# The third block of a causal convolution as four accumulating matrix products

## The chip, the cores and the metric

The kernel runs on one core of one Trainium2 chip. The metric is the device time in microseconds of one execution; the time of a kernel is the median of its runs. TensorE, VectorE, ScalarE and GpSimd work side by side, each through its own queue in order, and wait for one another by semaphores; SyncE issues the transfers.

## The reference

16 sequences of 64 tokens with 128 channels attend to 1601 context tokens each, go through a state-space layer and an MLP, and then through a mixture of eight experts. The change lies in the state-space layer, of which this matters:

```
v = layernorm(x, ln1_w, ln1_b)
zxbcdt = v @ in_proj_w.T                    # 128 -> z 256 | xBC 384 | dt 4
dt  = softplus(dt_raw + dt_bias)
xBC = sum(conv_w[:, k] * pad(xBC)[:, k:k+L] for k in range(4)) + conv_b   # causal, per channel
xBC = silu(xBC)                             # xs 256 | B 64 | C 64
h_t = exp(dt * A) h_{t-1} + dt * xs_t B_t ;  y_t = h_t C_t + D * xs_t
out = rmsnorm(y * silu(z)) @ out_proj_w.T
```

All arithmetic of this layer is in 32-bit floats. The channels of xBC come in three blocks of 128: two of xs, and a third with B in its first 64 rows and C in its last 64.

## The kernel before

The program has three blocks, one after the other: the attention (to about 400 us), the state-space layer with its MLP (function `mamba_mlp`, 400 to 475 us) and the experts. Each block writes out by hand, engine by engine, what the engine does in which order. `win` holds the input projection transposed (columns 0 to 255 z, 256 to 639 xBC, 640 to 643 dt), `vecs` per-channel columns (taps at `V_CW`, bias at `V_CB`), and `rows` a few vectors laid out over all 128 partitions.

In the second block the 1024 tokens are handled as two halves `h` of 512, each eight sequences of 64. Channels lie on the partitions. For each half, TensorE turns v (`turn_v`, L1159), ScalarE copies it to `vT` with scale and bias (L1354), and TensorE makes three products of 512 columns, one for each block of channels (`project_x`, L1164), each into one bank of the accumulator memory, named by `MM_BANK[h][c]`. ScalarE reads the bank, multiplies by the last tap, adds the bias and writes `conv` (`last_tap`, L1360); VectorE adds the three earlier taps, each shifted by one more token within its sequence, reading the bank again (`convolve`, L1541); ScalarE takes the silu into `xbc` (`conv_silu`, L1378), for the third block in two parts of 64 rows. TensorE's products for z (L1199, banks `Z_BANK`) feed `gate_silu` (L1383).

VectorE's order is: convolve (0,0) and (0,1), four small steps for dt, convolve (0,2), six steps, convolve (1,0), four steps, convolve (1,1), the decay split into three bf16 parts (L1590 to L1596), convolve (1,2), and then the train of `scan` (L1602), `mixed` (L1614, L1619) and `gated` (L1632). TensorE turns the decay parts (L1228) into banks 2 and 3, ScalarE copies them to `decayT` (L1400), TensorE spreads them over the partitions (`spread`, L1212), ScalarE copies the spread (`decay_all`, L1409) and VectorE scans it. `overlap` (L1240) multiplies B by C, `turn_x` (L1221) turns xs, `skipped` (L1254) starts the sums of y in banks 0 and 1 (first half) or 2 and 3 (second half) of the slots `YA_SLOT`, `state` (L1265) adds to them, and `project_out` (L1276, L1281) makes the output and the sums of squares.

Products called `idle` (L139) compute something that nobody reads; they only keep TensorE at work at chosen places. All their records have the line L139. `s["mm"]` counts finished projections, `s["tap"]` last taps, `s["conv"]` convolutions, `s["silu"]` silus, `s["zin"]` and `s["zsil"]` the gate's products and silus, `s["dp"]` parts of the decay, `s["dpt"]` their turning, `s["dpc"]` the copies to `decayT`, `s["bc"]` and `s["bcc"]` spreads and their copies, `s["ya"]` finished halves of y.

Of the kernel before, what the change touches and what calls it, by code (L numbers as in the profile page):

```python
# [5 lines left out]
ALU = mybir.AluOpType  # L6
ACT = mybir.ActivationFunctionType
# [4 lines left out]
P = 128  # L12
B, LQ, LK = 16, 64, 1601
# [27 lines left out]
V_CW, V_CB, V_D, V_NW, V_FCB = 9, 21, 24, 26, 28  # L41
# [1 line left out]
NV = 36  # L43

R_BV, R_BO, R_PB, R_ALOG, R_DTB = 0, 128, 256, 384, 388
NR = 392

MH = 4
E, NH, HT = 8, 3, 114
# [92 lines left out]
def attention(nc, A, keep):  # L142


    with ExitStack() as ctx:
# [97 lines left out]
        s_laid = sem("s_laid")  # L243
# [147 lines left out]
        def _(pool):  # L391
# [94 lines left out]
            for c in range(2):  # L486
                pool.tensor_scalar(keep.skip[:, c, :], keep.ident[:], keep.vecs[:, V_D + c:V_D + c + 1], None,
                                   ALU.mult).then_inc(s_laid, 1)
            for c in range(2):
                pool.tensor_scalar(keep.wout[:, c, :], keep.wout[:, c, :], keep.vecs[:, V_NW + c:V_NW + c + 1], None,  # L490
                                   ALU.mult).then_inc(s_laid, 1)
# [534 lines left out]
def mamba_mlp(nc, A, keep):  # L1026

    with ExitStack() as ctx:
# [9 lines left out]
        rows, vecs, ident = keep.rows, keep.vecs, keep.ident  # L1038
# [6 lines left out]
        vT = sb("vT", [P, T])  # L1045
        stats, mean_var, rstd12, var12 = keep.stats, keep.mean_var, keep.rstd12, keep.var12
        rstd = sb("rstd2", [P, NT])
        conv = sb("conv", [P, 4, T])
# [37 lines left out]
        def tok(t):  # L1086
            return slice(t * P, t * P + P)

        def half(h):
            return slice(512 * h, 512 * h + 512)  # L1090
# [5 lines left out]


        MM_BANK = ((2, 3, 4), (5, 0, 1))
        Z_BANK = ((4, 7), (6, 5))
        FC_BANK = ((2, 3, 4, 6), (7, 0, 1, 5))  # L1100
        TURN_BANK = (4, 6)

# [32 lines left out]
        def _(pe):  # L1135
# [27 lines left out]
            def project_x(h, c):  # L1163
                pe.matmul(bank(MM_BANK[h][c]), keep.win[:, 256 + P * c:256 + P * c + P], vT[:, half(h)],  # L1164
                          start=True, stop=True).then_inc(s["mm"], 1)

            def idle(b, times):
                spend(pe, bank(b), keep.w_hi[:, 0, 0, 0:P],
                      keep.w_hi[:, 1].rearrange("p g c -> p (g c)")[:, 0:512], times)
# [7 lines left out]
            project_x(0, 0)  # L1177
            project_tokens()
            project_x(0, 1)
            project_x(0, 2)  # L1180
            idle(1, 3)
            turn_v(0, 1, 1)
            idle(6, 4)
# [2 lines left out]
                last = pe.matmul(bank(6)[:, MH * t:MH * t + MH], vT[:, tok(t)], keep.win[:, 640:644],  # L1186
                                 start=True, stop=True)
            last.then_inc(s["dtp"], 1)
            for c in range(3):
                project_x(1, c)  # L1190
            for h in range(2):
                for c in range(2):

                    if c == 0:
                        pe.wait_ge(*((s["conv"], 3), (s["dts"], 2))[h])
                    elif h:
                        idle(3, 3)
                        pe.wait_ge(s["conv"], 4)
                    pe.matmul(bank(Z_BANK[h][c]), keep.win[:, P * c:P * c + P], vT[:, half(h)],  # L1199
                              start=True, stop=True).then_inc(s["zin"], 1)  # L1200

# [20 lines left out]
                last.then_inc(s["xt"], 1)  # L1222


            idle(3, 12)
            pe.wait_ge(s["dp"], 3)
            for t in range(NT):
                last = pe.matmul(ps[0:3 * MH, 1, tok(t)], decay_parts[:, t, :], ident_bf[:], start=True, stop=True)  # L1228
            last.then_inc(s["dpt"], 1)
            idle(0, 4)  # L1230
            pe.wait_ge(s["dpc"], 1)
            spread(0)

            def overlap(h):
# [10 lines left out]
            def skipped(h2):  # L1245

                if h2:
                    pe.wait_ge(s["bcc"], 4)
                else:
                    pe.wait_ge(s["conv"], 6)  # L1250
                pe.wait_ge(s["silu"], 4 * h2 + 2)
                for b in range(2):
                    for c in range(2):
                        pe.matmul(y_out(h2, b, c), keep.skip[:, c, :],  # L1254
                                  xbc[:, c, half(h2)].rearrange("p (t b q) -> p t b q", b=2, q=LQ)[:, :, b, :],
                                  start=(c == 0), stop=False, skip_group_check=True)
# [89 lines left out]
        def _(act):  # L1346
# [10 lines left out]
            def last_tap(h, c):  # L1357

                act.wait_ge(s["mm"], 3 * h + c + 1)
                nc.scalar.activation(conv[:, c, half(h)], bank(MM_BANK[h][c]), ACT.Identity,  # L1360
                                     bias=vecs[:, V_CB + c:V_CB + c + 1],
                                     scale=vecs[:, V_CW + 4 * c + 3:V_CW + 4 * c + 4]).then_inc(s["tap"], 1)
# [10 lines left out]
            def conv_silu(h):  # L1373

                for c in range(4):
                    act.wait_ge(s["conv"], 3 * h + min(c, 2) + 1)
                    m, src = (P, conv[:, c, half(h)]) if c < 2 else (64, conv[64 * (c - 2):64 * (c - 1), 2, half(h)])
                    nc.scalar.activation(xbc[0:m, c, half(h)], src, ACT.Silu).then_inc(s["silu"], 1)  # L1378

            def gate_silu(h):  # L1380
                for c in range(2):
# [4 lines left out]
            act.wait_ge(s["dts"], 4)  # L1386
            nc.scalar.activation(dt_e[:], dt_a[:], ACT.Exp).then_inc(s["dte"], 1)
            nc.scalar.activation(a_exp[:], rows[:, R_ALOG:R_ALOG + MH], ACT.Exp).then_inc(s["dte"], 1)
            last_tap(0, 2)
            last_tap(1, 0)  # L1390
            act.wait_ge(s["dts"], 5)
            nc.scalar.activation(dt_l[:], dt_u[:], ACT.Ln).then_inc(s["dte"], 1)
            last_tap(1, 1)
            last_tap(1, 2)
            act.wait_ge(s["dts"], DT_LAST - 1)
            nc.scalar.activation(decay[:], decay[:], ACT.Exp, bias=keep.marks[:, M_FIRST:M_FIRST + 1],
                                 scale=-1.0).then_inc(s["dts"], 1)
            conv_silu(0)
            act.wait_ge(s["dpt"], 1)
            nc.scalar.copy(decayT[:], ps[0:3 * MH, 1, :]).then_inc(s["dpc"], 1)  # L1400
            gate_silu(0)
            act.wait_ge(s["ones"], 1)
            for c in range(4):
# [42 lines left out]
        def _(dve):  # L1446
# [85 lines left out]

            def convolve(h, c):

                dve.wait_ge(s["tap"], 3 * h + c + 1)
                src = bank(MM_BANK[h][c]).rearrange("p (b q) -> p b q", q=LQ)
                dst = conv[:, c, half(h)].rearrange("p (b q) -> p b q", q=LQ)
                cw = vecs[:, V_CW + 4 * c:V_CW + 4 * c + 4]
                for k in range(1, 4):
                    settle()  # L1540
                    ins = dve.scalar_tensor_tensor(out=dst[:, :, k:], in0=src[:, :, 0:LQ - k],  # L1541
                                                   scalar=cw[:, 3 - k:4 - k], in1=dst[:, :, k:],
                                                   op0=ALU.mult, op1=ALU.add)
                    if k < 3:
                        count(ins)
                    else:
                        ins.then_inc(s["conv"], 1)
# [17 lines left out]
            step(dve.tensor_scalar(dt_a[:], dt_x[:], -1.0, None, ALU.mult))  # L1565
            step(dve.tensor_tensor(dt_a[:], dt_a[:], dt_x[:], ALU.min))
            step(dve.tensor_scalar(dt[:], dt_x[:], 0.0, None, ALU.max))
            convolve(0, 2)
            dve.wait_ge(s["dte"], 2)
            step(dve.tensor_scalar(dt_u[:], dt_e[:], 1.0, None, ALU.add))  # L1570
            step(dve.tensor_scalar(dt_a[:], dt_u[:], -1.0, None, ALU.add))
# [15 lines left out]
            for part in range(3):  # L1587
# [6 lines left out]
                    rest = decay_rest  # L1594
                else:
                    dve.tensor_copy(to, rest[:]).then_inc(s["dp"], 1)  # L1596
            convolve(1, 2)


            def scan(c):  # L1600
# [412 lines left out]
def program(nc, A, out):  # L2013
    with ExitStack() as ctx:
        def sb(name, shape, dt=F32):
            return ctx.enter_context(nc.sbuf_tensor("keep_" + name, shape, dt))

        keep = Keep()
        keep.x = sb("x", [P, NT, P])
        keep.ident = sb("ident", [P, P])  # L2020
        keep.marks = sb("marks", [P, 5])
        keep.vecs = sb("vecs", [P, NV])
        keep.rows = sb("rows", [P, NR])
        keep.iota = sb("iota", [P, E])
        keep.sums = sb("sums", [P, GH, T])
        keep.wo = sb("wo", [P, P])
        keep.win = sb("win", [P, 644])
        keep.wout = sb("wout", [P, 2, P])
        keep.wfc = sb("wfc", [P, 4 * P])
        keep.wproj = sb("wproj", [P, 4, P])  # L2030
        keep.w_hi = sb("w_hi", [P, E, 2, NH * HT], BF16)
        keep.w_lo = sb("w_lo", [P, E, 2, NH * HT], BF16)
        keep.delta = sb("delta", [P, 8, LQ])
        keep.skip = sb("skip", [P, 2, P])
        keep.sel = sb("sel", [3 * MH, MH, P], BF16)
        keep.ident_bf = sb("ident_bf", [P, P], BF16)
        keep.stats = sb("stats", [P, NT, 6])
        keep.mean_var = sb("mean_var", [P, NT, 2])
        keep.rstd12 = sb("rstd12", [P, 2, NT])
        keep.var12 = sb("var12", [P, NT])  # L2040
        attention(nc, A, keep)
        keep.tT = sb("tT", [P, T])
        keep.bgu = sb("bgu", [HT, E, 2, NH])
        keep.b2 = sb("b2", [E, P])
        keep.cent = sb("cent", [P, E])
        keep.cent_sq = sb("cent_sq", [P, E])
        keep.ones = sb("ones", [P, P])
        keep.norms = sb("norms", [P, NT])
        keep.dots = sb("dots", [P, 5 * E])
        keep.t_hi = sb("t_hi", [P, T], BF16)  # L2050
        keep.t_lo = sb("t_lo", [P, T], BF16)
        keep.w2 = sb("w2", [HT, E, NH, P])
        mamba_mlp(nc, A, keep)
        experts(nc, A, keep, out)

def lay_out(a):
# [20 lines left out]
    def cols(v):  # L2079
# [6 lines left out]
        cols(np.repeat(g["attn_D_param"], 64)), cols(g["attn_norm_w"]), cols(g["attn_fc_b"]),  # L2086
        np.where(marks[:, M_LOW:M_LOW + 1] > 0, bq.reshape(P, G), 0).astype(f)], 1)
    rows = np.concatenate([g["xattn_bv"], g["xattn_bo"], g["attn_proj_b"], g["attn_A_log"],
                           g["attn_dt_bias"]])[None]
    c = np.ascontiguousarray  # L2090
    return {
        "x": c(g["x"].reshape(T, P)),
# [36 lines left out]
```

## Time and profile before

| what | value |
|---|---|
| median of 3 runs | 590.32 us (589.23, 590.91, 590.32) |
| the profiled execution's own time | 589.35 us |
| its span, first to last instruction | 587.5 us |
| mean granted TensorE clock | 0.976 of full |
| busy: TensorE, VectorE, ScalarE, GpSimd | 89%, 71%, 65%, 55% |

The span is what the trace covers; 1.85 us of the execution's time lie around it. The trace shows for each engine when each instruction started and how long it took, and, where an engine stood idle, whose semaphore ended the wait. The granted clock is given as a share of TensorE's full 2.4 GHz; 0.50 is its lower level, 1.2 GHz.

### The profile page before, as it was taken

The page shows a single profiled execution, that of the slowest core. Times are in us where ns is not written, and L with a number is a line of the kernel's source. Part 1 is how long each engine was busy: PE and PEld are TensorE (multiplying, and loading weights), DVE is VectorE, ACT ScalarE, POOL GpSimd, SP SyncE. Part 2 cuts the span into 40 slices and gives each one's busy share as a digit, 9 for nine tenths or more (in the row PEclk, how much of TensorE's full clock was granted, in tenths as well). Part 3 has the DMA queues.
Part 4 walks back from the last instruction along what each step waited for, and adds up shares of the span by engine and source line. Part 5 has one row for each costly group of instructions (what it writes and reads, how often), then busy time and mean ns, then how long its engine had stood idle before and what let it go on. Part 6 is the DMA issues. An engine that isn't in the chain of part 4 may idle for free. (4 is left out here: it accounts for less than half of the span.)

```text
span 587.5 us, 18795 instructions
## 1 busy us (share of the span) xinstructions
PE 523.7 (89%) x7876; PEld 338.8 (58%) x7876; DVE 419.7 (71%) x751; ACT 381.1 (65%) x704; POOL 323.8 (55%) x197
## 2 busy tenths in 40 slices
PE   3988999999999889999999897998899868999996
PEld 1634555565565555665665564664367635777775
DVE  6277887788788786798798698536887576455555
ACT  4873667678677667677777677873672525666662
POOL 2697967558657556559558099303000035667772
PEclk9987999999999998999999999999899989999999
DMA  6897766684694682864762775002000000000001
GB/s 210 128 137 127 163 83 103 105 113 82 96 125 69 96 107 56 127 85 90 116 88 39 112 113 109 5 2 99 1 2 1 1 1 1 2 2 0 0 0 37
DMA packets 16409, 41.62 MB, mean 71 GB/s; under 512 B 3990, under 2 KB 6814, under 8 KB 16218
## 3 DMA queue, kind: packets, MB, share of 16 engines
q1 hardware_dynamic: 15592, 40.09, 41.9%
q8 instruction: 59, 0.97, 0.8%
q10 hardware_dynamic: 740, 0.42, 0.2%
q14 instruction: 18, 0.15, 0.1%
HBM read 19.70 MB, written 0.52 MB: 34 GB/s over the span
## 5 line engine op out<-in xcount | busy, mean ns | idle before, releaser
L896 DVE TENSOR_REDUCE half_max<-wide 128x2 f32<-128x802 f32 x256 | 241.8, 989 | 55.7 <-PE wide L582 51.9
L822 ACT ACTIVATE probs<-score 128x512 f32<-128x512 f32 (+1 forms) x416 | 225.8, 596 | 74.0 <-PE score L633 73.6
L653 PE MATMUL sums<-probs,values 128*32 128x192 f32 (+3 forms) x3328 | 133.6, 280 | 5.4 <-issue 5.3
L653 PEld LDWEIGHTS sums<-probs,values 128*32 128x32 f32 (+1 forms) x3328 | 87.5, 110 | 58.2 <-issue 30.4
L582 PE MATMUL wide<-k_stack,q_cur 48*128 48x401 bf16 x512 | 88.1, 340 | 12.6 <-ACT k_full L804 6.1
L633 PE MATMUL score<-q_cur,k_stack 50*128 50x128 bf16 (+1 forms) x1664 | 83.3, 219 | 9.5 <-ACT probs L822 4.7
L413 POOL TENSOR_TENSOR ctx_hi<-ctx_in,one 128x1601 bf16<-128x1601 f32 x15 | 42.9, 2859 | 76.5 <-PE wide L504 67.7
L1864 POOL TENSOR_TENSOR hid_lo<-hid_e,hid_hi 114x512 bf16<-114x512 f32 x47 | 54.2, 1158 | 36.6 <-ACT hid_hi L1892 35.5
L633 PEld LDWEIGHTS score<-q_cur,k_stack 50*128 50x128 bf16 (+1 forms) x1664 | 52.1, 95 | 35.4 <-issue 11.7
L1992 DVE SCALAR_TENSOR_TENSOR hid_e<-gu,keep_bgu,gate 114x512 f32<-114x512 f32 x48 | 35.9, 751 | 42.1 <-ACT gate L1905 40.7
L425 POOL TENSOR_TENSOR k_hi<-k_full,one 128x1601 bf16<-128x1601 f32 x15 | 42.9, 2857 | 41.9 <-ACT k_full L804 33.6
L1905 ACT ACTIVATE gate<-gu,gate_bias 114x512 f32<-114x512 f32 x48 | 32.9, 688 | 37.5 <-PE gu L1833 35.0
L416 POOL TENSOR_TENSOR ctx_lo<-ctx_in,ctx_hi 128x1601 bf16<-128x1601 f32 x15 | 48.6, 3242 | 1.2
L428 POOL TENSOR_TENSOR k_lo<-k_full,k_hi 128x1601 bf16<-128x1601 f32 x15 | 48.6, 3238 | 1.2
L582 PEld LDWEIGHTS wide<-k_stack,q_cur 48*128 48x128 bf16 x512 | 25.0, 94 | 39.1 <-DVE half_max L896 16.3
L1831 PE MATMUL gu<-keep_t_hi,keep_w_hi 128*114 128x512 bf16 x96 | 37.5, 390 | 6.6 <-DVE hid_e L1992 6.6
L804 ACT ACTIVATE k_full<-wide,keep_vecs 128x802 f32<-128x802 f32 x26 | 24.2, 930 | 25.6 <-PE wide L504 25.6
L892 DVE COPY values<-wide 128x896 f32<-128x896 f32 (+1 forms) x28 | 28.7, 1025 | 15.4 <-PE wide L504 15.4
L1833 PE MATMUL gu<-keep_t_hi,keep_w_lo 128*114 128x512 bf16 x96 | 37.1, 387 | 0.0
L1832 PE MATMUL gu<-keep_t_lo,keep_w_hi 128*114 128x512 bf16 x96 | 37.1, 386 | 0.0
L502 PE MATMUL wide<-wkv_hi,ctx_hi 128*128 128x128 bf16 x182 | 33.4, 225 | 2.9 <-DVE half_max L896 2.9
L1812 PE MATMUL down<-w_hi,hid_hi 114*128 (+1 forms) x192 | 33.8, 219 | 1.1 <-DVE hid_lo L2001 1.1
(310 smaller groups left out, 889.1 us busy)
## 6 DMA issues: line engine op xcount, KB each, us to landing
k_stack<-k_hi SPq DMA_DIRECT2D x64, 204.0 KB, 6.4
ctx_in<-in_ctx SPq DMA_DIRECT2D x56, 200.1 KB, 6.3
k_stack<-k_lo SPq DMA_DIRECT2D x32, 204.0 KB, 8.6
ctx_in<-in_wgu SPq DMA_DIRECT2D x16, 171.0 KB, 4.8
keep_w<-in_w SPq DMA_DIRECT2D x1, 1368.0 KB
ctx_in<-in_ctx SPq DMA_DIRECT2D x1, 800.5 KB, 8.2
keep_x<-in_x SPq DMA_DIRECT2D x1, 512.0 KB, 6.8
out<-keep_x SPq DMA_DIRECT2D x2, 256.0 KB, 2.4
```

The costliest lines, as they stand in the source:

```text
L413: pool.tensor_tensor(ctx_hi[:, n, 0:LK], ctx_in[:, n, :], one[:].to_broadcast([P, LK]), ALU.mult).then_inc(s_splithi, 1)
L416: pool.tensor_tensor(ctx_lo[:, n, 0:LK], ctx_in[:, n, :], ctx_hi[:, n, 0:LK], ALU.subtract).then_inc(s_split, 1)
L425: pool.tensor_tensor(k_hi[:, 0:LK], k_full[:, 0:LK], one[:].to_broadcast([P, LK]), ALU.mult).then_inc(s_khi, 1)
L428: pool.tensor_tensor(k_lo[:, 0:LK], k_full[:, 0:LK], k_hi[:, 0:LK], ALU.subtract).then_inc(s_klo, 1)
L582: last = pe.matmul(wide[:, w, 512 * p:512 * p + CH], q_cur[half:half + TERM, b % NQ, g].rearrange("p h q -> p (h q)"), k_stack[half:half + ...
L633: last = pe.matmul(score[0:m, (2 * step + p) % NSCORE, P * g:P * g + P], k_stack[half:half + TERM + 2, n, g, k * P:k * P + m], q_cur[half: ...
L653: last = pe.matmul(sums[32 * g:32 * g + 32, first * LQ:(first + heads) * LQ], values[0:m, n, k, VW * g + 2 * c:VW * g + 2 * c + 32], probs ...
L822: nc.scalar.activation(probs[0:m, step % NPROB, :].rearrange("r (g p c) -> r p g c", g=G, p=2)[:, p], score[0:m, (2 * step + p) % NSCORE, ...
L896: dve.tensor_reduce(half_max[:, b % 2, :, u // 4, u % 4], wide[:, w, :].rearrange("p (c k) -> p c k", c=2)[:, :, 0:CH], AX.X, ALU.max).the ...
L1831: pe.matmul(o, hi, t_hi[:, half], start=True, stop=False)
L1832: pe.matmul(o, hi, t_lo[:, half], start=False, stop=False)
L1864: pool.tensor_tensor(hid_lo[:, par, h, n, :], hid[:, n, :], hid_hi[:, par, h, n, :], ALU.subtract).then_inc(s["lo"], 1)
```

## The change

The third block of channels (B and C) is no longer convolved by ScalarE and VectorE. A new tensor `win_taps` holds four copies of its projection weights, each multiplied by one tap per output channel; GpSimd makes it in the attention block. TensorE then forms the convolved block itself: one product with the last tap over all 512 columns, and three that add the earlier taps, reading tokens shifted by one, two and three inside each sequence (504, 496, 488 columns). The silu reads that bank directly and adds the bias. The counts of `tap` and `conv` become two per half, and what waited for them is renumbered.

As bank 4 and bank 1 now hold the convolved blocks until the silus have read them, the first gate product moves from bank 4 to bank 3, the turned decay parts go to two groups of rows of bank 2 alone (and are copied in two instructions), the first skip products wait for the eighth silu instead of the sixth convolution, and the unread products go to bank 2 where they went to bank 3, ten of them instead of twelve ahead of the decay's turning. `rows` grows by 512 columns for the taps.

```diff
-NR = 392
+R_CW = 392
+NR = 904
...
+            pool.tensor_tensor(keep.win_taps[:], keep.win[:, 512:512 + P].unsqueeze(1).to_broadcast([P, 4, P]),
+                               keep.rows[:, R_CW:R_CW + 4 * P].rearrange("p (k c) -> p k c", k=4),
+                               ALU.mult).then_inc(s_laid, 1)
...
-        Z_BANK = ((4, 7), (6, 5))
+        Z_BANK = ((3, 7), (6, 5))
...
+            def convolve_states(h):
+
+                out = bank(MM_BANK[h][2])
+                by_batch = out.rearrange("p (b q) -> p b q", q=LQ)
+                tokens = vT[:, half(h)].rearrange("p (b q) -> p b q", q=LQ)
+                pe.matmul(out, keep.win_taps[:, 3, :], vT[:, half(h)], start=True, stop=False, skip_group_check=True)
+                for back in range(1, 4):
+                    last = pe.matmul(by_batch[:, :, back:], keep.win_taps[:, 3 - back, :], tokens[:, :, 0:LQ - back],
+                                     start=False, stop=(back == 3), skip_group_check=True)
+                last.then_inc(s["mm"], 1)
...
-            project_x(0, 2)
+            convolve_states(0)
...
-            for c in range(3):
+            for c in range(2):
                 project_x(1, c)
+            convolve_states(1)
             for h in range(2):
                 for c in range(2):
                     if c == 0:
-                        pe.wait_ge(*((s["conv"], 3), (s["dts"], 2))[h])
+                        pe.wait_ge(*((s["conv"], 2), (s["dts"], 2))[h])
                     elif h:
-                        idle(3, 3)
-                        pe.wait_ge(s["conv"], 4)
+                        idle(2, 3)
+                        pe.wait_ge(s["conv"], 3)
...
-            idle(3, 12)
+            idle(2, 10)
             pe.wait_ge(s["dp"], 3)
             for t in range(NT):
-                last = pe.matmul(ps[0:3 * MH, 1, tok(t)], decay_parts[:, t, :], ident_bf[:], start=True, stop=True)
+                at = 32 * (t // 4)
+                last = pe.matmul(ps[at:at + 3 * MH, 1, tok(t % 4)], decay_parts[:, t, :], ident_bf[:],
+                                 start=True, stop=True)
             last.then_inc(s["dpt"], 1)
             idle(0, 4)
-            pe.wait_ge(s["dpc"], 1)
+            pe.wait_ge(s["dpc"], 2)
...
-                    pe.wait_ge(s["conv"], 6)
+                    pe.wait_ge(s["silu"], 8)
...
             def conv_silu(h):
                 for c in range(4):
-                    act.wait_ge(s["conv"], 3 * h + min(c, 2) + 1)
-                    m, src = (P, conv[:, c, half(h)]) if c < 2 else (64, conv[64 * (c - 2):64 * (c - 1), 2, half(h)])
-                    nc.scalar.activation(xbc[0:m, c, half(h)], src, ACT.Silu).then_inc(s["silu"], 1)
+                    if c < 2:
+                        act.wait_ge(s["conv"], 2 * h + c + 1)
+                        nc.scalar.activation(xbc[:, c, half(h)], conv[:, c, half(h)], ACT.Silu).then_inc(s["silu"], 1)
+                        continue
+                    rows = slice(64 * (c - 2), 64 * (c - 1))
+                    act.wait_ge(s["mm"], 3 * h + 3)
+                    nc.scalar.activation(xbc[0:64, c, half(h)], bank(MM_BANK[h][2])[rows], ACT.Silu,
+                                         bias=vecs[rows, V_CB + 2:V_CB + 3]).then_inc(s["silu"], 1)
...
-            last_tap(0, 2)
             last_tap(1, 0)
...
-            last_tap(1, 2)
...
-            nc.scalar.copy(decayT[:], ps[0:3 * MH, 1, :]).then_inc(s["dpc"], 1)
+            for h in range(2):
+                nc.scalar.copy(decayT[:, half(h)], ps[32 * h:32 * h + 3 * MH, 1, 0:512]).then_inc(s["dpc"], 1)
...
-            convolve(0, 2)
...
-            convolve(1, 2)
```

## Rows read from the trace of the kernel before

**Rows 1.** The page: span and instructions.

```profile
span 587.5 us, 18795 instructions
```

**Rows 2.** Timeline of TensorE, head of the second block: start, duration, instruction, idle before.

```profile
407.39 0.81 PE L139 MATMUL ps<-keep_w_hi 128*128 128x512 bf16 x3
409.13 1.15 PE L1159 MATMUL ps<-keep_ident,v 128*128 128x128 f32 x4 [0.93 <-DVE v L1483]
412.95 2.82 PE L1164 MATMUL ps<-vT,keep_win 128*128 128x512 f32 x6
418.46 1.43 PE L1199 MATMUL ps<-vT,keep_win 128*128 128x512 f32 x2 [2.68 <-DVE conv L1541]
419.68 3.31 PE L1199 MATMUL pt<-vT,keep_win 128*128 128x512 f32 x4
427.02 0.61 PE L1228 MATMUL ps<-keep_ident_bf,decay_parts 128*12 128x128 bf16 x8
455.20 0.61 PE L1159 MATMUL ps<-keep_ident,v 128*128 128x128 f32 x4
```

**Rows 3.** Timeline of VectorE, the same stretch.

```profile
416.13 2.27 DVE L1541 SCALAR_TENSOR_TENSOR conv<-ps,keep_vecs,conv 128x504 f32<-128x504 f32 x3 [1.11 <-ACT conv L1360]
425.94 0.18 DVE L1596 CAST decay_parts<-decay_rest 128x32 bf16<-128x32 f32 x1
426.04 2.27 DVE L1541 SCALAR_TENSOR_TENSOR conv<-ps,keep_vecs,conv 128x504 f32<-128x504 f32 x3
430.14 1.23 DVE L1602 TENSOR_TENSOR_SCAN gain<-decay_all,keep_delta 128x512 f32<-128x512 f32 x1 [1.83 <-ACT decay_all L1409]
```

**Rows 4.** Windows of 1 us: busy time of the engines, then the granted clock.

```profile
420.00:421.00 1.00, 1.00 (x2) 0.35 (x2) 0.96 (x2) 0.98 (x2) 0.00 (x0) 0.50 0.00 0
...
422.00:423.00 1.00, 1.00 (x3) 0.24 (x2) 0.86 (x6) 0.12 (x1) 0.00 (x0) 0.72 0.00 0
```

**Rows 5.** Timeline of ScalarE.

```profile
427.67 1.00 ACT L1400 CAST decayT<-ps 12x1024 bf16<-12x1024 f32 x1 [0.83 <-PE ps L1228]
428.58 0.58 ACT L1383 ACTIVATE zg<-ps 128x512 f32<-128x512 f32 x1
429.07 0.57 ACT L1383 ACTIVATE zg<-pt 128x512 f32<-128x512 f32 x1
431.56 2.32 ACT L1378 ACTIVATE xbc<-conv 128x512 f32<-128x512 f32 x4
455.59 1.84 ACT L1434 ACTIVATE conv<-ps,keep_vecs 128x512 f32<-128x512 f32 x3
```

**Rows 6.** One line's records: duration least, median, most, in ns.

```profile
L1164 PE MATMUL ps<-vT,keep_win x12: 592/592/676, 404.4 to 415.2; 128*128 128x512 f32 x12
```

**Rows 7.** Timeline of TensorE, the train of scans and states, and one later row.

```profile
431.62 1.89 PE L1254 MATMUL ps<-xbc,keep_skip 128*128 128x256 f32 x8
433.44 0.44 PE L1212 MATMUL ps<-decayT,keep_sel 12*64 12x64 bf16 x16
435.84 0.69 PE L1265 MATMUL ps<-mix,keep_sums 64*64 64x64 f32 x32
458.16 1.13 PE L1323 MATMUL pt<-vT,keep_wfc 128*128 128x512 f32 x2 [1.49 <-ACT vT L1354]
```

**Rows 8.** Timeline of VectorE, the same stretch.

```profile
436.67 1.29 DVE L1632 TENSOR_TENSOR y<-ps,zg 128x512 f32<-128x512 f32 x2
443.99 0.16 DVE L1637 TENSOR_SCALAR rms<-ps 128x4 f32<-128x4 f32 x1 [2.11 <-PE ps L1281]
```

**Rows 9.** Timeline of GpSimd at the end of the attention block.

```profile
357.94 1.27 POOL L484 TENSOR_TENSOR keep_delta<-keep_ident 128x512 f32<-128x512 f32 x1
```

**Rows 10.** Load of the rows: issues, size, us from issue to landing.

```profile
keep_rows<-in_rows SPq DMA_DIRECT2D x1, 196.0 KB, 10.3
```

**Rows 11.** Windows of 2 us after that load: last the transfer share and GB/s.

```profile
68.00:70.00 2.00, 2.00 (x32) 1.03 (x28) 0.15 (x2) 1.38 (x3) 1.92 (x2) 1.00 0.58 120
70.00:72.00 2.00, 1.59 (x30) 0.79 (x22) 2.00 (x3) 1.59 (x4) 2.00 (x1) 1.00 0.01 3
```

More of the change, by code:

```diff
@@ L1533, in convolve @@
             def convolve(h, c):
-                dve.wait_ge(s["tap"], 3 * h + c + 1)
+                dve.wait_ge(s["tap"], 2 * h + c + 1)
                 src = bank(MM_BANK[h][c]).rearrange("p (b q) -> p b q", q=LQ)
@@ L2029, in program @@
         keep.wfc = sb("wfc", [P, 4 * P])
+        keep.win_taps = sb("win_taps", [P, 4, P])
         keep.wproj = sb("wproj", [P, 4, P])
@@ L2088, in lay_out @@
     rows = np.concatenate([g["xattn_bv"], g["xattn_bo"], g["attn_proj_b"], g["attn_A_log"],
-                           g["attn_dt_bias"]])[None]
+                           g["attn_dt_bias"], g["attn_conv_w"].reshape(3, P, 4)[2].T.reshape(-1)])[None]
     c = np.ascontiguousarray
```

## The prediction

> **What bounds the kernel now.** The page gives a span of 587.5 us [rows 1] and TensorE busy 89% of it, but such shares are means over three stages, and the change touches only the middle one, the state-space layer and its MLP (400 to 475 us). The chain of waits is no help here: it ends at the block boundary at 474.97 us, so I read the timelines of the engines one beside the other, looking for which wait ends last.
>
> TensorE's timeline of the head of the stage [rows 2]: it has issued the second half's products by 415.7, then idles 2.68 us for conv (VectorE's third convolution, which begins late, at 416.13, because ScalarE's last tap of that block stands behind the Exp [rows 3]). Just after it resumes at 418.46 the granted clock is half: 0.50 of full speed in the slice from 420, and 0.72 as a mean in that from 422, when it is back [rows 4]. That is the 1.2 GHz level. The records of the gate products show it: four take 3.31 us, where six of the same shape took 2.82 [rows 2]. The low stretch, some 3.4 us from about 419.1 to 422.6, costs 1.7 us of matmul work. Then come twelve spare products and only at 427.02 the transposes of the decay. VectorE had finished the three parts of the decay at 426.12 [rows 3] (the semaphore reads little later), so it did not set the start of these transposes; TensorE itself did. From them ScalarE copies decayT (427.67), makes the gate, copies the first spread (429.55 to 430.11), and the scan begins at 430.14 [rows 3, 5].
>
> From the scan on, VectorE has no gap until 441.87 and each of its steps stands on the last. The end of this stretch, the first request for the rms at 443.99, waits for TensorE's output products [rows 8]. So two things set the stage's end: when the transposes of decay start, and then the train of scans, mixes and states.
>
> **The head: what is removed, what is added.** Removed from VectorE are two convolutions of three steps, 2.27 us each (2.19 from start to the next start) [rows 3]; from ScalarE two last taps of about 0.7 us. The second of the two convolutions, 426.04 to 428.31, lay before VectorE's wait until 430.14, so it is worth nothing. The first stood in the decay's own path, and with its wait of 1.11 us held the next steps from 415.01 to 418.32 (416.13 + 2.19). They now begin when ScalarE's a_exp is done, 415.37 and a handover, say 415.42. That is 2.90 us earlier: convolution (1,0) ends near 419.1, the three parts of decay near 423.2. ScalarE follows: it has a table load, Ln, a table load and Exp in the same order; its silus end near 423.9.
>
> Added on TensorE: a half's third product was one float product of 512 columns (two records, 0.85 us). It is now four, of 512, 504, 496 and 488 columns: 0.85 + 0.84 + 0.83 + 0.81 = 3.33 us, so 2.48 us more, twice. I follow the queue:
> - first half: the spare products at 407.39 begin at 409.87, and three of them end at 410.52. The turning of v began at 409.13 and had to wait for its last tile until 409.9; without waits it takes 0.61, as the row at 455.20 shows. So it ends about 411.15 instead of 410.28, so vT, the dt products and the second half's products move by 0.86 [rows 2]. The dt product ends near 413.95; VectorE asks for it at 414.17, so this delay is covered with 0.2 us to spare.
> - second half: the first of the four tap products starts at 414.75 + 0.86 = 415.61 (the six records before end at 415.77 [rows 2] and one lasts 0.59 [rows 6], so the last starts at 415.18 and the fifth, where the change's product stands, at 414.75) and the four end at 418.94.
> - gate products: the wait is now for conv 2, long met, and conv 3 (419.1). Three at 0.85 end at 421.50, three spare products at 422.15, the last gate product at 423.00, ten spare ones (0.215 each) at 425.15. The parts of decay are ready at 423.2. So the transposes start at 425.16, not 427.02: 1.86 us earlier. In this count TensorE has no long idle between 412 and 425, and I take the full clock.
> - the copy of decayT becomes two of 512 columns. The one of 1024 occupied ScalarE 0.91 us up to the next start; two like the gate's cost 0.49 each [rows 5]: 0.07 more.
>
> The head gains 1.86 - 0.07 = 1.79 us. A rule of the Trainium skill (ScalarE: Activation LUTs, What ACT_TABLE_LOAD costs) makes each per-partition bias pointer 93 ns dearer, and the two silus per half now have one. It would add some 0.2 us per half. The rows first: a silu from SBUF without such a bias came each 0.58 us (four in 2.32), a Gelu from PSUM with bias not later (three in 1.84, 0.61 at most) [rows 5], so I add nothing; the sum can do without the rule.
>
> **The tail: the new wait.** The products of the skip term go into banks 0 and 1. Bank 1 is now read by ScalarE's last two silus of the second half, so skipped(0) waits for silu 8, not for conv 6. Before, it started at 431.62, while these silus ran from 431.56 to 433.88 [rows 5, 7]. ScalarE runs without a gap from 427.67 to there, so in this train's own time silu 8 stays at 433.88, and skipped(0) can start at 433.93: 2.31 us later. Queued behind it on TensorE are spread(2), turn_x(2) and (3), overlap(1), state(0) and (1), spread(3), state(2) and (3). Who waits: spread(2) goes from 433.44 to 435.75; its copy and turn_x make the dtx of tiles 2 and 3 end near 437.2 and the third scan, at 1.2 us, 438.4. State(3) ends at 436.53 + 2.31 = 438.84. The gating waits for it; it began at 436.67 [rows 8], so it now begins 2.2 us later: before it followed state(3) by 0.14. Behind it skipped(1) ends near 441.1, just when the dtx of tile 5 ends, so the loss stays between 2.2 and 2.3. I take 2.25. Nothing later takes it back: the rms request at 443.99 hangs on this train.
>
> **Others at nothing.** The weights times taps, 128x512 float on GpSimd: delta of the same size took 1.27 us [rows 9]; it lies at about 360, ahead of the last two expert splits, which only the block's end waits for; the engine ends at 373 and next works at 401.55, so 27 us of cover; without them 1.3 us. The rows' load grows from 196 to 452 KB at 57.9 us. The load took 10.3 us to land among the others [rows 10]. The DMA share falls from 0.58, at 120 GB/s, to 0.01 in the slice from 70 [rows 11]; 256 KB at that rate are 2.1 us, which fit there. Uncovered they could hold a batch's load by that, 2 us at most.
>
> **The sum.** -1.79 + 2.25 = +0.46 us on the profiled span: 587.96. The profiled execution took 589.35 us, 1.85 around its span, so 589.8; it lies 0.97 below the median 590.32 of the three runs. On that median's scale: 590.8.
>
> **The rivals.**
> 1. *The clock falls in the new wait (slower).* In the tail's new order TensorE has about 0.9 us without work before turn_x(0), then 0.66 us of turns, then 2.2 us without work. The head of before shows 2.68 us idle followed by half clock [rows 4]; the gap of 1.49 us before 458.16 shows none: its pair of records took 1.13 us, the pair at 418.46 took 1.43 [rows 2, 7]. The new stretch is between these. It decides if the clock falls from 431 to 433.5 in the new run: then the 4.9 us of TensorE work from skipped(0) to state(3), which now bounds everything, lies partly at half clock. A low stretch of 3.4 us as in [rows 4] costs 1.7 if it lies wholly in this work, and 1.0 if it begins 1.2 us before it: 591.8 to 592.5, likeliest 592.2. Chance 0.30, as the gap is broken by work. The Trainium skill (TensorE: Matmul & The Clock Gate, What's actually happening) also has recent idleness halve the clock; by that, the trace agrees with its 0.50.
> 2. *The tail loses nothing (faster).* If TensorE catches up before the gating, the head's 1.79 us stay: 588.5. Against it: TensorE's timeline is full from 433.44 to 436.53 and VectorE's from 430.14. Chance 0.12.
> 3. *The head gives less.* The strided reads of the tap products may be slower than 0.43 us: the skip's records, strided too, came each 0.228 against 0.213 at full rate, 7%, which on 6.7 us is 0.45. Also, not each of the runs before need have had the low clock of 419; without it the gate products end 1.7 earlier, the decay's parts (426.1) become the bound, and the transposes gain only 0.99 against such a run. The first alone gives +0.9, the second alone +1.3: 591.2 to 591.6. Chance 0.13.
> 4. *The sum as it stands*: 590.8, chance 0.45.
>
> **How the numbers follow.** A measurement of this kernel can tell about 0.3%, 1.8 us, from no change, so faster means below 588.5 and slower above 592.1. Faster: half of rival 2, whose 588.5 is the bound itself, and 0.04 for a head that gains more than I count: 0.10. Slower: two thirds of rival 1 (0.20), 0.05 of rival 3 (both its parts at once, 592.1), 0.05 of case 4 (a transfer of [rows 11] uncovered): 0.30. Same: 0.60. The range reaches from rival 2 to the likeliest of rival 1 and the transfer and stride bounds beyond it: 588.4 to 592.6; the likeliest case's own is 590.0 to 591.5.
>
> **What would show each step.** Right: decay's transposes about 1.9 us earlier; no half clock from 412 to 428; ScalarE's decayT near 425.8; an idle of 2.2 us of TensorE ended by ScalarE's xbc silu; the gating of y near 437.1. Wrong: transposes waiting for dp or a clock below 1.00 in the head; skipped(0) followed by a gating no later than 435.5; records of the skip at 0.43 us each (rival 1); taps' records over 0.45 us each (rival 3).

## The result and the profile after

The changed kernel is slower. In the first set it took 594.87 us (median of six runs, 593.64 to 598.12) against 590.23 of the kernel before: a ratio of 1.0107, 95% interval 1.007 to 1.0143. Two later sets of twelve gave 1.0043 (1.0002 to 1.0085) and 1.0082 (1.0044 to 1.012); the kernel before against itself gave 1.0004 (0.9975 to 1.0032). So the loss is real, and its size, 2.1 to 6.6 us between the medians of a set, varies with the executions. The forecast was 590.8, range 588.4 to 592.6.

The page of the changed kernel, its span and the granted clock by fortieths of it:

```profile
span 591.7 us, 18808 instructions
...
PEclk9888999999999999999999998999979978999999
```

A slice is 14.8 us. The 7 of the 30th, 429 to 444 us, is the first of two low stretches; the second falls into the 33rd, from 473, and runs over to that of the experts' start, which the kernel before has too. TensorE's timeline (start, duration, instruction, idle before), which answers to [rows 2] and [rows 7]:

```profile
406.87 2.66 PE L1178 MATMUL ps<-vT,keep_win_taps 128*128 128x504 f32 x6
409.37 0.81 PE L140 MATMUL ps<-keep_w_hi 128*128 128x512 bf16 x3
410.01 0.60 PE L1163 MATMUL ps<-keep_ident,v 128*128 128x128 f32 x4
...
418.45 1.02 PE L1215 MATMUL ps<-vT,keep_win 128*128 128x512 f32 x2
...
424.78 0.40 PE L1245 MATMUL ps<-keep_ident_bf,decay_parts 128*12 128x128 bf16 x8
...
429.05 0.66 PE L1237 MATMUL pt<-keep_ident,xbc 128*128 128x128 f32 x4 [0.91 <-ACT zg L1406]
432.03 3.75 PE L1272 MATMUL ps<-xbc,keep_skip 128*128 128x256 f32 x8 [2.32 <-issue]
435.71 0.63 PE L1228 MATMUL ps<-decayT,keep_sel 12*64 12x64 bf16 x16
...
438.69 0.69 PE L1283 MATMUL ps<-mix,keep_sums 64*64 64x64 f32 x32
...
475.76 2.82 PE L140 MATMUL ps<-keep_w_hi 128*128 128x512 bf16 x7
```

VectorE (answering to [rows 3] and [rows 8]):

```profile
402.05 0.29 DVE L1515 RECIPROCAL o_rden<-ps 128x24 f32<-128x24 f32 x1
...
422.60 0.18 DVE L1617 CAST decay_parts<-decay_rest 128x32 bf16<-128x32 f32 x1
428.03 1.22 DVE L1622 TENSOR_TENSOR_SCAN gain<-decay_all,keep_delta 128x512 f32<-128x512 f32 x1 [5.25 <-ACT decay_all L1431]
...
436.99 0.78 DVE L1639 TENSOR_TENSOR keep_sums<-pt,dt 128x256 f32<-128x256 f32 x2 [4.20 <-PE pt L1237]
...
439.52 1.29 DVE L1652 TENSOR_TENSOR y<-ps,zg 128x512 f32<-128x512 f32 x2 [0.62 <-PE ps L1283]
...
479.06 0.43 DVE L1940 CAST keep_t_hi<-keep_tT 128x512 bf16<-128x512 f32 x1 [2.05 <-PEq L1032]
```

ScalarE (answering to [rows 5]):

```profile
425.24 1.18 ACT L1422 CAST decayT<-ps 12x512 bf16<-12x512 f32 x2 [1.64 <-PE ps L1245]
426.44 0.60 ACT L1406 ACTIVATE zg<-ps 128x512 f32<-128x512 f32 x1
...
430.55 1.38 ACT L1400 ACTIVATE xbc<-ps,keep_vecs 64x512 f32<-64x512 f32 x2
```

Windows of 2 us (busy time of TensorE, its weight loads, VectorE, ScalarE, GpSimd, then the granted clock), answering to [rows 4]:

```profile
428.00:430.00 2.00, 0.79 (x14) 0.44 (x6) 1.83 (x3) 1.98 (x5) 0.00 (x0) 1.00 0.03 8
430.00:432.00 2.00, 0.00 (x0) 0.00 (x1) 2.00 (x4) 1.90 (x4) 0.00 (x0) 0.57 0.01 4
432.00:434.00 2.00, 1.97 (x5) 1.63 (x6) 0.76 (x3) 0.00 (x0) 0.00 (x0) 0.50 0.00 0
```

The reader is to see four things. The head did its part: taps in records 0.42 to 0.43 us apart, no idle ahead of the gate products, the turning of the decay 424.78. Then TensorE stands idle 2.32 us; the profile names no releaser, but what the first skip products wait for in the kernel, the eighth silu, ends at 431.93 (430.55 + 1.38). In this execution the clock falls to 0.50 inside that wait, at 430.3, and the eight skip records take 3.75 us where they took 1.89. VectorE waits 4.20 us for the turned xs behind them. And at the block's end the seven unread products take 2.82 us, again at half clock; VectorE waits 2.05 us for the block to close.

The attention block ends at different times from one execution to the next, so I compare by distances from the first reciprocal of the middle block, the row at 402.05 above. In the first trace of the kernel before it is

```profile
402.56 0.29 DVE L1493 RECIPROCAL o_rden<-ps 128x24 f32<-128x24 f32 x1
```

Worked out so from the timelines of fourteen profiled executions (us behind that reciprocal; "decay turned" is the start of the turning on TensorE, "first scan" and "gating" the first scan and the first product of y with the gate on VectorE, "next block" the first cast of the experts' block there; "low clock" lists where the 1 us windows show under 1.00 between 412 and 479, in time of the trace):

| execution | reciprocal at | decay turned | first scan | gating | next block | low clock |
|---|---|---|---|---|---|---|
| before | 402.56 | 24.46 | 27.58 | 34.11 | 72.41 | 419-423 |
| before, second | 402.53 | 23.62 | 26.74 | 34.86 | 73.17 | 431-435 |
| changed | 402.05 | 22.73 | 25.98 | 37.47 | 77.01 | 430-438, 474-479 |
| changed, second | 401.89 | 22.73 | 25.99 | 36.94 | 75.23 | 428-436 |
| changed, third | 400.27 | 22.74 | 25.99 | 36.92 | 75.22 | 427-435 |
| wait filled late | 402.10 | 22.74 | 25.99 | 36.40 | 76.17 | 429-434, 474-478 |
| wait filled, both gaps | 401.66 | 22.74 | 25.99 | 35.09 | 74.70 | 473-477 |
| early silus | 402.61 | 22.73 | 25.99 | 32.55 | 70.84 | none |
| early silus, second | 405.07 | 22.74 | 25.99 | 32.55 | 71.68 | 474-479 |
| before, wait for silu 8 | 401.03 | 24.46 | 27.58 | 40.45 | 81.54 | 417-421, 431-445 |
| changed, shorter pad at the end | 400.80 | 22.73 | 25.99 | 37.52 | 75.74 | 429-436, 473-479 |
| decay turned early | 403.09 | 20.80 | 24.39 | 34.21 | 73.68 | 427-435, 472-476 |
| decay turned early, filled | 401.15 | 20.81 | 24.39 | 31.97 | 71.06 | 470-477 |
| early silus, filled | 403.27 | 22.73 | 25.98 | 32.54 | 71.91 | 472-479 |

Each run reports its mean clock too; (1 - clock) x 2 x time is its time at 1.2 GHz. Over all 30 runs of the changed kernel, those included that the comparisons leave out as disturbed, it is 38.7 us with a mean time of 594.3; over 139 of the kernel before 31.8 and 589.6. Straight lines fitted through the runs rise by 0.36 and 0.28 us of time for each us at the low level and, drawn out to no time at the low level, where no run lies, come to 580.4 and 580.8 us.

### The profile page after: what moved, and what is told of

Its sections match the earlier page's. It is cut to its first block and busy times, and to the rows that moved or that the text cites. A ratio compares the mean times of both kernels' runs of the same rounds, so it can differ in the third digit from the quotient of the medians.

```text
span 591.7 us, 18808 instructions
## 1 busy us (share of the span) xinstructions
PE 526.8 (89%) x7886; PEld 341.4 (58%) x7886; DVE 415.8 (70%) x745; ACT 380.3 (64%) x703; POOL 325.0 (55%) x198
## 5 line engine op out<-in xcount | busy, mean ns | idle before, releaser
L826 ACT ACTIVATE probs<-score 128x512 f32<-128x512 f32 (+1 forms) x416 | 225.8, 596 | 75.8 <-PE score L637 75.5
L506 PE MATMUL wide<-wkv_hi,ctx_hi 128*128 128x128 bf16 x182 | 32.1, 221 | 2.9 <-DVE half_max L900 2.9
```

Source lines behind the costliest of these rows:

```text
L826: nc.scalar.activation(probs[0:m, step % NPROB, :].rearrange("r (g p c) -> r p g c", g=G, p=2)[:, p], score[0:m, (2 * step + p) % NSCORE, ...
```

## The experiments

**The changed kernel again**, twice.

> The changed kernel unaltered, for its own spread and as the measure for the other three. Theory 1 (the wait for the eighth silu, and TensorE's clock falling inside it) expects in its trace again a granted clock of 0.50 from about 1.2 us after the turning of xs to the third spread, skip records of about 0.43 us cadence, and a median 4 to 5 us above the kernel before. Theory 2 (the low clock in that place is chance; the extra time comes from several low stretches anywhere, above all the one at the block's end that begins at 474 us) expects a trace in which the stretch after the turning of xs is at 1.00, with the median still 4 us above.

1.0043; its trace has the low stretch from 428.9 (0.94 in that window, then 0.50):

```profile
428.89 1.12 PE L1237 MATMUL pt<-keep_ident,xbc 128*128 128x128 f32 x4 [0.91 <-ACT zg L1406]
431.87 3.75 PE L1272 MATMUL ps<-xbc,keep_skip 128*128 128x256 f32 x8 [1.86 <-issue]
```

Theory 2 fell, and of Theory 1 the skip records came true, but not the start: the clock fell as the turning of xs began (its records took 1.12 us, where the first trace has 0.66), ahead of the new wait and not 1.2 us behind the turning. The median was 2.1 us above the kernel before, not 4 to 5. The block closed at full clock, so the second low stretch belongs to some executions only.

> The changed kernel a third time, beside the kernel before on the same chip, since the two sets of runs so far gave 1.011 and 1.004. Theory 1 expects 0.4 to 1.1% above, the turning at 22.7, the gating between 36.9 and 37.6 (35.1 only if the clock happened to stay full), the low stretch starting between 427 and 431.5.

1.0082, gating 36.92, low from 427.2, again ahead of the wait:

```profile
427.28 1.12 PE L1237 MATMUL pt<-keep_ident,xbc 128*128 128x128 f32 x4 [0.91 <-ACT zg L1406]
```

**The wait filled late.** One line:

```diff
             pe.wait_ge(s["ones"], 1)
+            idle(0, 10)
             skipped(0)
```

> Ten unread products (2.15 us) stand between the turning of xs and the wait of the first skip products; nothing else changes, and the eighth silu still comes after them. Theory 1 expects the clock to stay at 1.00 there, the eight skip records to take 1.9 us instead of 3.75, the gating of y to begin 2.5 to 3 us earlier than in the changed kernel, and a median 2.5 to 4 us below it: within 0.3% of the kernel before. Theory 2 expects less than 1 us. If the products themselves hold up the skip products, the trace shows these starting later than the eighth silu.

Ratio 1.0012 (0.9984 to 1.004), median 592.29, as that of the changed kernel beside it (592.31); the means are 591.8 and 593.5. TensorE's timeline:

```profile
429.11 0.66 PE L1237 MATMUL pt<-keep_ident,xbc 128*128 128x128 f32 x4 [0.91 <-ACT zg L1407]
429.88 3.73 PE L140 MATMUL ps<-keep_w_hi 128*128 128x512 bf16 x9
433.45 1.89 PE L1272 MATMUL ps<-xbc,keep_skip 128*128 128x256 f32 x8
```

The expectation of a full clock failed: it fell at 429.7 (0.87 in the window from 429), just ahead of the fill, and the unread products, planned at 2.15 us, took 3.7 and themselves held up the skip products past the silu. So the fall came before these products could begin; the low stretch was 3.4 us long, though, where the changed kernel's are 6.8.

**Both gaps filled**: four unread products ahead of the first turning of xs as well, and nine in the wait.

> The changed kernel with unread products in both gaps before the first skip products: four (0.86 us) ahead of the first turning of xs, nine (1.94 us) behind it; the wait for the eighth silu stays. Theory 1, that the low clock comes of the thin work between the spreads and the skip products, expects 1.00 from 426 to 440 us, skip records in 1.9 us, and the gating of y 2.2 to 2.4 us later than in the kernel with the early silus (so 34.8 to 35.0 us after the stage's first reciprocal, against 32.55 there, 34.11 in the kernel before, 36.9 to 37.5 in the changed one): the wait's own price without the clock's. Median 0 to 1.5 us above the kernel before. If the clock falls all the same, activity in this stretch is not what decides and the gating comes past 36.

TensorE, then VectorE, then windows of 2 us of this kernel:

```profile
429.16 2.10 PE L140 MATMUL ps<-keep_w_hi 128*128 128x512 bf16 x9
431.60 1.99 PE L1272 MATMUL ps<-xbc,keep_skip 128*128 128x256 f32 x8 [0.34 <-ACT xbc L1402]
```

```profile
436.75 1.29 DVE L1654 TENSOR_TENSOR y<-ps,zg 128x512 f32<-128x512 f32 x2 [0.50 <-PE ps L1283]
```

```profile
428.00:430.00 2.00, 2.00 (x11) 0.98 (x11) 1.87 (x4) 1.98 (x5) 0.00 (x0) 1.00 0.03 8
430.00:432.00 2.00, 1.67 (x8) 0.77 (x7) 1.97 (x4) 1.52 (x3) 0.00 (x0) 1.00 0.02 4
432.00:434.00 2.00, 2.00 (x25) 1.50 (x24) 0.42 (x2) 0.00 (x1) 0.00 (x0) 1.00 0.00 0
```

The same wait for the same silu, and the clock stays at 1.00: the gating comes at 35.09, not 36.9 to 37.5. That parts the two costs, by one trace. The ratio is 1.001 (0.9974 to 1.0046), the median 1.8 us above the kernel before, a little more than expected; this execution had the low stretch at the block's end.

**The early silus**: the wait taken away by its cause.

```diff
             conv_silu(0)
+            conv_silu(1, (2, 3))
             act.wait_ge(s["dpt"], 1)
...
                 if c == 1:
-                    conv_silu(1)
+                    conv_silu(1, (0, 1))
...
-                    pe.wait_ge(s["silu"], 8)
-                pe.wait_ge(s["silu"], 4 * h2 + 2)
+                    pe.wait_ge(s["silu"], 6)
+                pe.wait_ge(s["silu"], (2, 8)[h2])
```

> ScalarE makes the second half's two silus of the third block right behind the first half's, in the 1.64 us in which it waits for the turned decay, so the skip products wait for the sixth silu, which is long done. Theory 1 expects no idle before the skip products, clock 1.00, the whole loss of the tail gone (2.3 us of wait and the clock's part), and only the gain of the head left: 1 to 2 us below the kernel before, some 6 below the changed kernel. Theory 2 expects it to stay 2 us or more above the kernel before, since the end of the block is as it was.

```profile
429.61 0.66 PE L1237 MATMUL pt<-keep_ident,xbc 128*128 128x128 f32 x4 [0.91 <-ACT zg L1406]
430.10 1.89 PE L1272 MATMUL ps<-xbc,keep_skip 128*128 128x256 f32 x8
```

No idle, no low clock; gating at 32.55, 1.56 us ahead of the kernel before's first trace. Ratio 0.9951 (0.9923 to 0.998). The median, 587.97, is 4.3 us below that of the changed kernel beside it, not some 6.

> The kernel with the early silus a second time, beside the version above on the same chip. Expected again some 2 us below the kernel before, and its trace without a low clock between 412 and 440. If its gain was the first chip's chance, it lies within 0.3% of the kernel before now, and its trace shows a low stretch there.

The second time 0.9992 (0.9964 to 1.0021), with the same 32.55 in the trace and nothing low between 412 and 440, so both of its alternatives were half right: the block is faster, the run's gain is at the edge of what can be measured. This execution had a low stretch from 474.

**One part of the change alone**: the kernel before with `pe.wait_ge(s["silu"], 8)` for `pe.wait_ge(s["conv"], 6)`.

> The kernel before with one part of the change alone: the first skip products wait for the eighth silu instead of the sixth convolution. Everything else is as before, so the result is the same output. Theory 1 expects the gating of y 2.2 us later if the clock stays full, 3 to 5 us later if it falls, as it does in the changed kernel; the median 2 to 5 us above the kernel before. If the cost lies in the four tap products or the larger transfer instead, this kernel is not slower than before by more than 1 us.

1.0087 (1.0054 to 1.012), median 596.33.

```profile
432.45 3.75 PE L1254 MATMUL ps<-xbc,keep_skip 128*128 128x256 f32 x8 [2.21 <-issue]
...
440.21 1.13 PE L1265 MATMUL ps<-mix,keep_sums 64*64 64x64 f32 x32
```

The wait alone makes the loss, without taps, larger load or new order of the head. It was larger than expected: the median 6.1 us above the kernel before for 2 to 5, the gating 6.3 us later for 3 to 5. In this execution the low stretch lasted from 431 to 445.

**The kernel before again.**

> The kernel before against itself: what this measurement calls no change, and a second trace of its middle block. Theory 1 expects a ratio of 1.000 within 0.004; decay's turning 24.46 us and the gating 34.1 us after the stage's first reciprocal if the clock falls at the gate products as in the first trace, both about 0.9 us earlier if it does not; and no low clock between 424 and 440. If a low stretch in the scans appears here too, the new wait is not what brings it.

```profile
426.15 0.61 PE L1228 MATMUL ps<-keep_ident_bf,decay_parts 128*12 128x128 bf16 x8 [0.34 <-DVE decay_parts L1596]
...
430.26 0.66 PE L1221 MATMUL pt<-keep_ident,xbc 128*128 128x128 f32 x4 [0.86 <-ACT zg L1383]
430.75 3.28 PE L1254 MATMUL ps<-xbc,keep_skip 128*128 128x256 f32 x8
```

The ratio was as expected, the trace not. The head kept its clock and the turning came 0.84 earlier, as rival 3 had it. But a low stretch from 431.1 took the skip products, without the new wait. So the clock can fall at this place without the new wait, as it did in one of the two traces of the kernel before, for 3.4 us. The three traces of the changed kernel, and a fourth with a shorter pad further on, all have the fall, and it lasts 6.8 us in each. In two of them it came at 428.9 and 427.2, before the new wait began. Up to there TensorE's rows stand at the same distances in the kernel with the early silus (the turning of xs 27.00 behind the reciprocal in each), and its two traces show no fall. So the wait did not bring these two falls; that it makes the low stretch more frequent or longer fits the counts and the mean clocks, but these few traces don't show it (the early decay's trace, below, has 6.8 us without this wait).

**The decay turned early**: early silus, one unread product instead of ten, the early silus moved behind the second half's gate.

> The kernel with the early silus, with one unread product instead of ten ahead of the decay's turning, and the two early silus moved behind the gate's second half so that they don't hold up the copy of the decay. The decay's parts are ready near 422.8, the turning started at 424.8 behind the products. Theory 1 expects the turning 1.9 us earlier, the scan 1.4 to 1.7 us earlier, no low clock, and a median 1 to 2 us below that of the early silus (3 to 5 below the kernel before). If the products are needed to hold the clock, the trace shows 0.50 between 426 and 436 and the gain is gone.

```profile
423.89 0.40 PE L1245 MATMUL ps<-keep_ident_bf,decay_parts 128*12 128x128 bf16 x8
...
428.49 1.11 PE L1237 MATMUL pt<-keep_ident,xbc 128*128 128x128 f32 x4 [0.91 <-ACT zg L1406]
429.96 3.75 PE L1272 MATMUL ps<-xbc,keep_skip 128*128 128x256 f32 x8 [0.35 <-issue]
```

The turning came 1.93 earlier (20.80), and the clock fell at 427.9: gating at 34.21, later than the early silus' 32.55; ratio 0.9985 (0.9951 to 1.0019). The two silus, now behind the gate, also end late, at 429.85, and the skip products wait for them. That the products removed there were what held the clock is suggested by this one trace, not shown.

> The kernel with the early decay's turning, its gaps filled with unread products: seven instead of four behind the turning, four ahead of the first turning of xs, three ahead of the first skip products. In the version without them the turning came 1.9 us earlier, but the clock fell at 427 and the gating was 1.7 us later than with the early silus alone. Theory 1 expects 1.00 throughout from 412 to 440, the gating at 30.9 to 31.3 us after the stage's first reciprocal (32.55 with the early silus alone, 34.11 in the kernel before), and a median 2 to 4 us below the kernel before. If the clock falls still, the gating is at 33 or later and the median no better than the early silus.

Filled again, the clock held in this block up to 470, but the gating came at 31.97 instead of 31.1. The two silus stand ahead of the second copy of the spread on ScalarE, which costs the second scan 0.25 us; and they end only at 427.91, so the skip products start 2.42 us behind the first scan, at 427.96, where the early silus have 1.50, and the gating then waits 0.50 us for TensorE. Ratio 0.9993 (0.9962 to 1.0023): nothing that can be measured.

**A shorter pad at the end of the block**, three unread products for seven, in the changed kernel.

> The changed kernel with three unread products instead of seven at the end of the block. In its profile these seven ran at half clock for 2.8 us and were the last to finish in the block. If that second low stretch carries a regular part of the loss, the median falls by 0.5 to 1.5 us against the changed kernel; in its trace the next block begins within 0.9 us of VectorE's last step instead of 2.05. If the low stretch at the end is chance and rare, or the next block then starts at half clock, no difference.

```profile
475.00 1.06 PE L140 MATMUL ps<-keep_w_hi 128*128 128x512 bf16 x2 [0.22 <-issue]
476.35 1.84 PE L1804 MATMUL small<-keep_cent,keep_tT 128*128 128x8 f32 x8 [0.30 <-PEq L1032]
```

1.0042 (1.0006 to 1.0077), as the changed kernel had in another set: no difference shown. The pad is shorter, and VectorE waits 0.72 us for the next block instead of 2.05, but that block began at half clock.

**The last gap filled**: early silus, with four unread products ahead of the first turning of xs.

> The kernel with the early silus, with four unread products in the one gap that is left ahead of the first turning of xs. The kernel before showed a low clock after this thin stretch in its second trace, the two traces of the early silus did not. If that stretch lowers the clock in some of their executions, this version's mean over its runs is 0.5 to 1 us below theirs (588.1 and 588.8) and the mean clock of its runs higher; if not, nothing is gained, and the gating stays at 32.5 us after the stage's first reciprocal.

587.51 us, ratio 0.9952 (0.9923 to 0.9981), the lowest of all; gating 32.54. The mean of its runs is 587.1, 1.0 and 1.7 below those of the early silus, and the mean clock 0.9747 against 0.9747 and 0.9711. Across different sets this is an indication only. That it beats the kernel before is measured in one set; the early silus alone had 0.9951 in one set and 0.9992 in the next, so a second set may give less here too. Its trace has a low stretch from 472 to 483.

## Why the prediction was wrong

**The bound and the head: right.** The turning of the decay moved by 24.46 - 22.73 = 1.73 us (1.86 forecast), in the first trace without idle up to it and without low clock from 412 to 428. The tap products ran at full rate in spite of their strides, so that part of rival 3 falls; the other, that the first trace's low clock in the head is not in every run, is confirmed by the second trace. The copies were mis-sized: two occupy ScalarE 1.20 us (425.24 to 426.44), not 0.98. The head gained 1.60, not 1.79. Silus with bias from PSUM cost 0.1 us more per half than I took (421.17 to 423.60 is 2.43, against 2.32); the estimate of 0.2 from the Trainium skill's 93 ns per pointer operand (ScalarE: Activation LUTs, What ACT_TABLE_LOAD costs) erred to the other side by about as much.

**The wait's own price: right in mechanism, low in size.** Both gaps filled against early silus, both at full clock: 35.09 - 32.55 = 2.54 us, for 2.25. The sum without the clock would have been -1.60 + 2.54 = +0.9 for +0.46.

**The step that failed** is the choice of the likeliest case: "the sum as it stands", at full clock. I put a fall of the clock in the new wait at 0.30 "as the gap is broken by work", and at 1.0 to 1.7 us (the lower end is 1.1 by its own terms, half of 3.4 less 1.2). It came in all three traces, cost 1.8 to 2.4 us at the gating (36.92 to 37.47 less the 35.09 of the one trace of this order at full clock), and lasted 6.8 us, not the 3.4 that I carried over from the head of the kernel before. What I weighed was the length of idle gaps, 2.68 against 1.49; the runs show that the spreads, overlaps and turns around them, short products with pauses, are no shield: the clock fell at 427.2 (third trace) and 429.7 (wait filled late) in executions where no idle longer than 0.91 us had yet come, and at 431.1 in the second trace of the kernel before, which has no such wait. So the cause that I gave the fall, the new wait, holds at most for the first trace and for the length; what decides when the clock falls here stays open.

**What I had not on the list** is the second low stretch. For the first trace: -1.60 + 2.54 + 2.38 at the gating (3.36 measured), 1.24 at the block's end (next block less gating: 39.54 against 38.30), 0.1 behind it and -0.5 from the attention make the 4.2 us between the spans. The second and third traces lack the 1.24. The shorter pad gave no gain. Of the fourteen traces neither of the kernel before has such a stretch, but the second of the early silus and that of the filled early silus, the fastest kernel, do, so I can't say that the change brings it.

**What stays open:** how often each stretch falls, and so why the sets gave 0.4 to 1.1%. Against the mean of the two traces of before (72.8) the three changed ones (75.8) lose 3.0 us in the block, while the means of the runs differ by 4.8. The 6.9 us more at the low level, at 0.3 us each, are 2 of these, and the wait's price of about 1 comes on top; the rest is not placed. The attention block's own length, 400.3 to 405.1 over the traces, moves each run by more. The larger load and GpSimd's product (1.28 us at 358.8) show nowhere; they were not tried by themselves.

## What to carry to other kernels

When a buffer passes from one reader to another, look at where the new reader stands in its queue: two silus that could have run in an idle stretch of ScalarE stood behind two others, and the price, 2.5 us of wait and some 2 of clock, was near three times what the head gained. A wait on TensorE can be priced twice, once as time and once as clock; look at the work ahead of it, not at the gap alone. And an unread product is only cheap at full clock: put in after the clock had fallen, ten of them took 3.7 us for the 2.15 planned, and became the delay themselves. In the three traces with four such products ahead of the first turning of xs the clock held there; so did it in the first of the kernel before and in two without them, so this is a place to try, not a proven cure.

## What the runs showed of the hardware

The granted clock fell to 0.50 with TensorE partly at work: in the changed kernel's third trace at 427.2, after 0.44, 0.68 and 0.44 us of short products from 424.70 to 426.37 and within an idle of 0.91 us; in the second trace of the kernel before at 431.1, while turns and skip products had run without a pause since 430.26 and the longest idle shortly before was 0.86 us. The Trainium skill (TensorE: Matmul & The Clock Gate, What's actually happening) has the clock set by how busy the engine has been recently, and names idleness as what lowers it; these traces agree with the first and show the fall after thin work too. The same kernel differs from run to run by up to 11 us (588.4 to 599.6), and the time at the low level, worked out from the reported mean clock, goes with it: their correlation is 0.92 over the 30 runs of the changed kernel and 0.75 over the 139 of before.
